# Stacks of the split heads by three transfers to every fourth partition, with zero rows between

## The chip, the cores and the metric

One Trainium2 chip, one NeuronCore. The time is the device time of one execution in microseconds; the median of three runs of the kernel before is 1024.43 us (1022.36 to 1027.62).

## The reference, cut to what matters

The input is 16 sequences of 256 tokens with 128 channels, float32. Two blocks follow each other, each on a layer norm of its input and added back to it: a gated linear attention block with a gated MLP, and a small graph of six attention nodes. The graph is the part that the stacks serve:

```python
for c in range(NUM_NOD):                      # 6 nodes, each reads up to 3 earlier ones
    q = ew[c, 0] * (nodes[in_q] @ We[eq] + be[eq])
    k = ew[c, 1] * (nodes[in_k] @ We[ek] + be[ek])
    v = ew[c, 2] * (nodes[in_v] @ We[ev] + be[ev])
    # _mha: 8 heads of 16 channels, 256 x 256 scores per head and sequence
    scores = jnp.einsum('bqhd,bkhd->bhqk', q @ wq, k @ wk) / jnp.sqrt(dh)
    ctx = jnp.einsum('bhqk,bkhd->bqhd', jax.nn.softmax(scores), v @ wv)
    nodes[c] = act_w[c] * (ctx @ wo) + q
```

## The kernel before

Five engines run hand-ordered programs and meet on semaphores. The first stage, `slots(eng, first, ...)`, does layer norm, linear attention and MLP for the 32 tiles of 128 tokens, four tiles an iteration, eight iterations, overlapped over four (`f`, `i`, `k`, `j`). The second stage, `node_slots(phase)`, does 96 steps, one for each node and sequence (`STEPS`). A step passes through stages at fixed distances in slots: projection of q and k (`a`), scores (`s`, 3 slots later), maxima (`m`, 4), weights (`x`, 5), values and output (`d`, 6). Between the first stage and the steady node stage the first four steps are woven into the last iterations.

**What a stack is.** The products of q and k need more precision than one pass of the float32r type has. So ACT copies q and k with their biases into `qk` (L784, L785), POOL splits each into a high and a low part in `hl` (L591, L594: `K_HI, Q_LO, K_LO, Q_HI`), and SP copies the parts into `st`, where three blocks of 16 channels lie under each other: high by high, high by low, low by high. One matmul over the 48 rows of a half sums the three. There are two halves, partitions 0 to 47 and 64 to 111, of one head each, and four pairs `j` along the free dimension. Partition `64 s + 4 d + j` of `hl` holds channel `d` of head `(j, s)`; a transfer takes the 64 partitions of one half to 16 partitions of `st`, so a stack is six transfers of 128 KB, all issued by SP in `stack` (L506). `st` has `STACKS = 6` buffers of 128 x 2048 float32, `hl` two; `stacked[r]` counts the landings and is awaited by POOL's `split` (two steps later, ahead of L591) and by PE's `scores` (k = 0). PE reads a stack in `scores` and in `weights`, in which a product of `ones` and `mst` of 64 rows subtracts the row maxima first. The matmuls are all recorded at L1292, the helper `mm`.

**The start.** POOL begins with memsets and four loads: `ones`, `mst`, small columns, then `qbd` (L548), `keT` (L549), `kvs` (L550), `am` (L551), each with a semaphore increment; then it waits for `const_in` and casts the identity (L553). Its first work of the first stage is the product of L565. DVE meanwhile takes the statistics of the first four tiles (L919, L1031), adds the epsilons in two tensor-scalars on 128 x 4 (L939, L940), after which ACT takes the inverse roots (L774, L776), DVE refines them and writes the normed rows (L974), and PE transposes them (L1391). PE fills its gaps at the start with dummy products of `ones` (`warm`).

Of the kernel before, what the change touches and what calls it, by code (L numbers as in the profile page):

```python
# [10 lines left out]
F32 = mybir.dt.float32  # L11
# [5 lines left out]
P = 128  # L17
# [20 lines left out]
H, DH = 8, 16  # L38
# [7 lines left out]
JH = H // 2  # L46
HALF = P // 2
PARTS = 3
KROWS = PARTS * DH
MROW = 3  # L50
MCOLS = 2 * MROW * JH
MSTEP = 24
# [6 lines left out]
STACKS = 6  # L59
# [70 lines left out]
def build(nc, a, consts, out):  # L130
    ds = bass.ds
    with ExitStack() as ctx:
# [46 lines left out]
        st = [sb(f"st{r}", [P, JH, 2 * T], F32R) for r in range(STACKS)]  # L179
        hl = [sb(f"hl{n}", [P, 4, T], F32R) for n in range(2)]  # L180
# [114 lines left out]
        def chain(name, events):  # L295
# [4 lines left out]
        L = names("x_first x_half x_in const_in wa_in gk_in wo_in mlp_in cols_in nodew_in wout_in scal_in ln_in")  # L300

        S = names("wa_ok we_t we_c fold_ps fold_ok be_c "
                  "bias_w wz_ok am0 pads_ok eps_ok one_ok ones_ok heads_ok scaled_ok prep_d")

        A = names("xn_ok h_ok hT_ps hT_ok z_ps b_ps eb_ok qkp_ps qke_ok qbd_ok "
                  "v_ps v_ok g_ps eg_ok sg_ok keT_ps keT_ok kv_ps am_ok "
# [22 lines left out]
        stacked = [sem(f"stacked{r}") for r in range(STACKS)]  # L329
# [90 lines left out]
        def unit(k):  # L420

            return k // 2, k % 2
# [45 lines left out]
        @block.sync  # L468
        def _(sp):

            sp.dma_start(xall[:, 0:TPI, :], x_d[:, 0:TPI, :]).then_inc(L["x_first"], 16)
            sp.dma_start(cst[:, :], consts).then_inc(L["const_in"], 16)
            sp.dma_start(wa[:, 0:QK], a["L0_attn_Wq"]).then_inc(L["wa_in"], 16)
            sp.dma_start(wa[:, QK:2 * QK], a["L0_attn_Wk"]).then_inc(L["wa_in"], 16)
            sp.dma_start(wa[:, 2 * QK:2 * QK + D], a["L0_attn_Wv"]).then_inc(L["wa_in"], 16)
            sp.dma_start(wa[:, 2 * QK + D:], a["L0_attn_Wg"]).then_inc(L["wa_in"], 16)
            sp.dma_start(wo[:, :], a["L0_attn_Wo"]).then_inc(L["wo_in"], 16)
            sp.dma_start(wgu[:, 0, :], a["L0_attn_W_gate"]).then_inc(L["mlp_in"], 16)
            sp.dma_start(wgu[:, 1, :], a["L0_attn_W_up"]).then_inc(L["mlp_in"], 16)
            sp.dma_start(wd[:, 0:2, :], a["L0_attn_W_down"][0:256, :].rearrange("(m p) d -> p m d", p=P)).then_inc(L["mlp_in"], 16)  # L480
            sp.dma_start(wd[0:MROWS[2], 2, :], a["L0_attn_W_down"][256:MLP, :]).then_inc(L["mlp_in"], 16)
            sp.dma_start(xall[:, TPI:TILES // 2, :], x_d[:, TPI:TILES // 2, :]).then_inc(L["x_half"], 16)
            sp.dma_start(be_rows, a["L0_ffn_be"]).then_inc(L["nodew_in"], 16)
            sp.dma_start(we_raw, a["L0_ffn_We"].rearrange("e d n -> d e n")).then_inc(L["nodew_in"], 16)
            for j, w in enumerate(("Wq", "Wk", "Wv")):
                sp.dma_start(wqkv_raw[:, j, :, :], a["L0_ffn_" + w].rearrange("c d n -> d c n")).then_inc(L["nodew_in"], 16)
            sp.dma_start(wo_raw, a["L0_ffn_Wo"].rearrange("c d n -> d c n")).then_inc(L["nodew_in"], 16)
            sp.dma_start(xall[:, TILES // 2:, :], x_d[:, TILES // 2:, :]).then_inc(L["x_in"], 16)
            for h in range(H):
                at = VW * (h % GCOL) + DH * (h // GCOL)  # L490
                sp.dma_start(w_out[at:at + DH, :, :], a["L0_ffn_Wo"][:, DH * h:DH * h + DH, :].rearrange("c d n -> d c n")).then_inc(L["wout_in"], 16)


            def stack(a):

                r, old = a.n % STACKS, at_slot(a.n, STACKS)
                if old is not None:
                    sp.wait_ge(B["x_ps"], old.n * UNITS + UNITS)
                for blk, (k, q) in enumerate(((K_HI, Q_HI), (K_HI, Q_LO), (K_LO, Q_HI))):
                    if blk == 0:  # L500
                        sp.wait_ge(B["hi_ok"], a.n + 1)
                    if blk == 1:
                        sp.wait_ge(B["lo_ok"], a.n + 1)
                    for s in range(2):
                        to = HALF * s + DH * blk
                        sp.dma_start(st[r][to:to + DH, :, :].bitcast(F32),  # L506
                                     hl[a.n % 2][HALF * s:HALF * s + HALF, k:q + 1:q - k, :].bitcast(F32))\
                            .then_inc(stacked[r], 16)

            def maxima_rows(m):  # L510

                old = at_slot(m.n, 2)
                if old is not None:
                    sp.wait_ge(B["x_ps"], old.n * UNITS + UNITS)
                else:
                    sp.wait_ge(S["ones_ok"], 3)
                sp.wait_ge(B["mt_ok"], m.n + 1)
                sp.dma_start(mst[m.n % 2][0:(2 * MROW - 1) * MSTEP + 1:MSTEP, :, :], mrows[m.n % 2][:, :]).then_inc(m_in[m.n % 2], 16)

            def phase(t, a, s, m, x, d, z, w, v):  # L520
                if m is not None:
                    maxima_rows(m)
                if at_slot(t, 1) is not None:
                    stack(at_slot(t, 1))

            for t in range(EARLY):
                phase(*stages(t))
            node_slots(phase)
            for f in range(LATE, BATCH):
                for t in range(KT):  # L530
                    sp.wait_ge(E[f - LATE]["done"], t + 1)
                    sp.dma_start(out_d[f][:, t:t + 1, :], xall[:, f * KT + t:f * KT + t + 1, :]).then_inc(B["last_stored"], 16)
            sp.wait_ge(B["last_stored"], 16 * KT * (BATCH - LATE))
# [3 lines left out]
        def _(pool):  # L537
# [11 lines left out]
            pool.memset(keT, 0.0).then_inc(S["pads_ok"], 1)  # L549
            pool.memset(kvs, 0.0).then_inc(S["pads_ok"], 1)  # L550
            pool.memset(am, 0.0).then_inc(S["am0"], 1)  # L551
            pool.wait_ge(L["const_in"], 16)
            pool.tensor_copy(identb[:, :], ident).then_inc(S["ones_ok"], 1)  # L553

# [29 lines left out]
            def split(a):  # L584

                to = hl[a.n % 2]
                old = at_slot(a.n, 2)
                if old is not None:
                    pool.wait_ge(stacked[old.n % STACKS], 96 * old.uses(STACKS))
                pool.wait_ge(B["qk_ok"], a.n + 1)  # L590
                pool.tensor_tensor(to[:, K_HI::Q_HI - K_HI, :], qk[a.n % 2], one_col[:, :].unsqueeze(2).to_broadcast([P, 2, T]), ALU.mult)\  # L591
                    .then_inc(B["hi_ok"], 1)
                pool.wait_ge(B["hi_ok"], a.n + 1)
                pool.tensor_tensor(to[:, K_LO:Q_LO - 1:-1, :], qk[a.n % 2], to[:, K_HI::Q_HI - K_HI, :].bitcast(F32), ALU.subtract)\  # L594
                    .then_inc(B["lo_ok"], 1)
# [694 lines left out]
        def _(pe):  # L1290
# [292 lines left out]
            def scores(s, k):  # L1583

                qt, g = unit(k)
                r = s.n % STACKS
                if k == 0:
                    pe.wait_ge(stacked[r], 96 * s.uses(STACKS))
                if s.n + S_AT < EARLY:
                    if 2 * k + 1 >= len(FIRST_RING):  # L1590
                        pe.wait_ge(B["max_ok"], 2 * k + 2 - len(FIRST_RING))
                else:
                    for e in range(2):
                        banks_free(s.n + S_AT, "s", k, e)
                for n in range(2):
                    for e in range(2):
                        rows, j = slice(HALF * e, HALF * e + KROWS), 2 * g + n
                        i = mm(s_bank(s, k, e)[:, n * T:n * T + T], st[r][rows, j, T + qt * P:T + qt * P + P], st[r][rows, j, 0:T])
                        if n == 1:
                            i.then_inc(B["s_ps"], 1)  # L1600

            def weights(x, k):

                g, kt = unit(k)
                r = x.n % STACKS
                if k == 0:
                    pe.wait_ge(m_in[x.n % 2], 16 * x.uses(2))
                for e in range(2):
                    rows = slice(HALF * e, HALF * e + HALF)
                    banks_free(x.n + X_AT, "x", k, e)  # L1610
                    mm(x_bank(x, k, e)[:, :].rearrange("p (j q) -> p j q", j=2), ones[rows, :], mst[x.n % 2][rows, 2 * g:2 * g + 2, :], stop=False, skip=True)
                for n in range(2):
                    for e in range(2):
                        rows, j = slice(HALF * e, HALF * e + KROWS), 2 * g + n
                        i = mm(x_bank(x, k, e)[:, n * T:n * T + T], st[r][rows, j, kt * P:kt * P + P], st[r][rows, j, T:2 * T],
                               start=False, skip=True)
                        if n == 1:
                            i.then_inc(B["x_ps"], 1)
# [114 lines left out]
```

## Time and profile before

| | us |
|---|---|
| median of 3 runs | 1024.43 |
| the profiled execution | 1026.44 |
| its span, first to last instruction | 1024.6 |
| PE busy | 975.5 |
| DVE busy | 836.5 |
| ACT busy | 724.2 |
| POOL busy | 449.1 |
| mean granted clock of TensorE, of full speed | 0.984 |

The span is what the trace covers; the execution's own time is 1.8 us longer. Busy times overlap, and matmuls are pipelined, so a row's duration is not what one matmul adds. L12 is line 12 of the kernel, PE is TensorE's matmul, PEld its weight load, DVE VectorE, ACT ScalarE, POOL GpSimd, SP the engine that issues the stacks. The first stage lasts until about 250 us, the node stage from there to the end.

### The profile page before, as it was taken

How to read it: one execution, taken by the hardware profiler on the slowest of the kernel's cores; microseconds unless marked ns; L12 is line 12 of the kernel's file. 1: busy time of each engine (PE TensorE's matmuls, PEld its weight loads, DVE VectorE, ACT ScalarE, POOL GpSimd, SP SyncE). 2: the span in 40 equal slices, each digit the busy share in tenths (PEclk: the TensorE clock that was granted, in tenths of full speed). 3: DMA queues.
4: the chain of work that ended last, by engine and by line, in shares of the span. 5: the costliest groups of instructions: out<-in, count | busy, mean ns of one | idle time of the engine just before them, and what ended most of it. 6: DMA issues, size and time to landing. Idle time of an engine off the chain costs nothing.

```text
span 1024.6 us, 26783 instructions
## 1 busy us (share of the span) xinstructions
PE 975.5 (95%) x9705; PEld 698.4 (68%) x9705; DVE 836.5 (82%) x1805; ACT 724.2 (71%) x1602; POOL 449.1 (44%) x874
## 2 busy tenths in 40 slices
PE   7989999998799999999999999999999999999995
PEld 4765656555577777777777777677777777777773
DVE  5466777765689998888888899988888888888896
ACT  3345666655477777787787778878777777787775
POOL 4522222224343334434444348854434435544355
PEclk9889999999899999999999999999999999999998
DMA  9100000003676667767676677876767767767641
GB/s 235 36 1 0 2 0 0 0 1 48 87 111 102 96 100 111 106 106 110 102 111 109 99 113 114 118 110 109 110 99 113 108 101 111 106 105 110 103 70 38
DMA packets 72407, 87.33 MB, mean 85 GB/s; under 512 B 11642, under 2 KB 45950, under 8 KB 72286
## 3 DMA queue, kind: packets, MB, share of 16 engines
q1 hardware_dynamic: 70686, 83.69, 53.1%
q0 software_dynamic: 800, 1.98, 1.1%
q8 instruction: 76, 1.25, 0.7%
q14 instruction: 45, 0.37, 0.2%
q10 hardware_dynamic: 800, 0.05, 0.1%
HBM read 6.90 MB, written 2.10 MB: 9 GB/s over the span
## 4 chain that ended last, share of the span: by engine, by line
PE 75%; DVE 10%; ACT 6%; issue 5%; POOL 3%; DMA 0%; DVEq 0%; ACTq 0%; POOLq 0%
PE bank L1292 73%; ACT region L820 2%; DVE region L1158 1%; DVE region L1090 1%; PE bank L1629 1%; POOL hl L591 1%; DVE region L974 1%; DVE region L1085 1%; POOL out L664 1%; ACT region L796 1%; DVE region L1078 1%; DVE region L1039 1%; DVE region L1070 1%; ACT region L690 0%; DVE region L939 0%
## 5 line engine op out<-in xcount | busy, mean ns | idle before, releaser
L1158 DVE TENSOR_REDUCE region<-bank 128x2 f32<-128x512 f32 x768 | 489.2, 679 | 82.4 <-PE bank L1292 80.6
L820 ACT ACTIVATE region<-bank 128x512 f32<-128x512 f32 x768 | 406.4, 599 | 29.8 <-PE bank L1292 18.6
L1292 PE MATMUL bank<-st 48*128 48x256 f32 x3072 | 310.4, 326 | 5.7 <-DVE region L1158 4.7
L1292 PEld LDWEIGHTS bank<-st 48*128 48x128 f32 x3072 | 243.6, 189 | 20.4 <-DVE region L1158 5.7
L591 POOL TENSOR_TENSOR hl<-qk,one_col 128x512 fp32r<-128x512 f32 x96 | 100.1, 1043 | 358.2 <-ACT qk L785 358.2
L1292 PE MATMUL bank<-region 128*32 128x256 f32 (+3 forms) x3554 | 250.0, 377 | 2.2 <-ACT region L820 0.7
L1292 PEld LDWEIGHTS bank<-region 128*32 128x32 f32 (+2 forms) x3554 | 130.8, 117 | 85.4 <-issue 16.5
L1292 PE MATMUL bank<-mst,ones 64*128 64x512 bf16 x768 | 150.4, 386 | 0.0
L594 POOL TENSOR_TENSOR hl<-qk,hl 128x512 fp32r<-128x512 f32 x96 | 123.7, 1288 | 7.5
L842 ACT ACTIVATE mrows<-bank 24x256 bf16<-24x256 bf16 x96 | 35.8, 373 | 125.9 <-PE bank L1629 125.9
L1292 PEld LDWEIGHTS bank<-mst,ones 64*128 64x128 bf16 x768 | 37.1, 92 | 55.6 <-ACT region L820 26.3
L1165 DVE STREAM_TRANSPOSE cst<-bank 128x512 f32<-128x512 f32 x96 | 67.6, 704 | 6.2 <-PE bank L1292 6.2
L1292 PE MATMUL bank<-xT,w_fold 128*128 128x256 f32 x192 | 63.3, 426 | 0.0
L1292 PE MATMUL bank<-region,w_fold 128*128 128x256 f32 x192 | 56.2, 388 | 0.0
L1292 PE MATMUL bank<-region,w_out 128*128 128x256 f32 x160 | 55.9, 431 | 0.0
L784 ACT ACTIVATE qk<-bank,bcol 128x256 f32<-128x256 f32 x96 | 47.5, 495 | 9.3 <-PE bank L1292 9.3
L1292 PEld LDWEIGHTS bank<-w_fold,region 128*128 128x128 f32 x320 | 47.4, 191 | 3.5
L1292 PE MATMUL bank<-region,wgu 128*128 128x512 f32 (+1 forms) x96 | 47.0, 601 | 2.0 <-DVE region L1085 1.3
L1292 PE MATMUL bank<-w_fold,region 128*128 128x128 f32 x320 | 48.6, 274 | 0.0
L785 ACT ACTIVATE qk<-bank,bcol 128x256 f32<-128x256 f32 x96 | 48.2, 502 | 0.0
L1169 DVE TENSOR_TENSOR region<-cst,region 128x256 f32<-128x256 f32 x96 | 41.0, 427 | 3.3
L834 ACT ACTIVATE region<-bank 128x256 f32<-128x256 f32 x96 | 38.5, 401 | 5.9 <-PE bank L1292 5.9
(194 smaller groups left out, 1267.9 us busy)
## 6 DMA issues: line engine op xcount, KB each, us to landing
st<-hl SPq DMA_DIRECT2D x576, 128.0 KB, 4.4
out<-xall POOLq DMA_DIRECT2D x14, 128.0 KB, 4.1
mst<-mrows SPq DMA_DIRECT2D x96, 12.0 KB
xall<-in_L_attn_hidden_states SPq DMA_DIRECT2D x1, 768.0 KB, 8.2
cst<-in_constants SPq DMA_DIRECT2D x1, 514.5 KB, 4.1
xT<-in_L_ffn_Wq SPq DMA_DIRECT2D x1, 384.0 KB
xT<-in_L_ffn_Wk SPq DMA_DIRECT2D x1, 384.0 KB
xT<-in_L_ffn_Wv SPq DMA_DIRECT2D x1, 384.0 KB
```

What stands on the lines that cost most here:

```text
L591: pool.tensor_tensor(to[:, K_HI::Q_HI - K_HI, :], qk[a.n % 2], one_col[:, :].unsqueeze(2).to_broadcast([P, 2, T]), ALU.mult)\
L594: pool.tensor_tensor(to[:, K_LO:Q_LO - 1:-1, :], qk[a.n % 2], to[:, K_HI::Q_HI - K_HI, :].bitcast(F32), ALU.subtract)\
L664: pool.dma_start(out_d[v.f], xall[:, v.f * KT:v.f * KT + KT, :]).then_inc(B["out_stored"], 16)
L784: act.activation(qk[a.n % 2][:, 0, :], bank[IN][:, 0:T], ACT.Identity, bias=bcol[:, a.c, 1:2])
L785: act.activation(qk[a.n % 2][:, 1, :], bank[IN][:, T:2 * T], ACT.Identity, bias=bcol[:, a.c, 0:1]).then_inc(B["qk_ok"], 1)
L820: act.activation(to, x_bank(x, k, e)[:, :].rearrange("p (j q) -> p j q", j=2), ACT.Exp).then_inc(B["exp_ok"], 1)
L834: act.activation(v[:, :, :, 0:DH], bank[IN][:, 0:T].rearrange("p (k h d) -> p k h d", k=KT, h=H), ACT.Copy).then_inc(B["vals_ok"], 1)
L842: act.activation(mrows[m.n % 2][:, :], bank[IN][0:MCOLS, 0:P].bitcast(BF16), ACT.Copy).then_inc(B["mt_ok"], 1)
L1158: dve.tensor_reduce(mx[s.n % 2][:, to:to + 2], s_bank(s, k, e)[:, :].rearrange("p (j k) -> p j k", j=2), AX_X, ALU.max, negate=True).then_ ...
L1165: dve.transpose(outT, bank[OUT][:, :]).then_inc(B["outT_ok"].sem, 1)
L1169: dve.tensor_tensor(ctxc.rearrange("p (b g d) -> p g b d", g=2, d=DH), blocks[:, :, :, 0:DH], rec.rearrange("p (g b) -> p g b", g=2).unsqu ...
L1292: return pe.matmul(o, w, x, start=start, stop=stop, skip_group_check=skip)
```

## The change

The three blocks of a stack no longer lie under each other. Block `blk` goes to partitions `blk, blk + 4, ..., blk + 124`, so one transfer serves both halves: 128 source partitions of `hl` to 32 partitions of `st`, 256 KB, three of them a stack. Every fourth partition from 3 on is written by none of them; POOL sets all six buffers to zero once, at the start, and SP waits for that ahead of the first use of each buffer. The matmuls run over all 64 rows of a half. The counts of `stacked` fall from 96 to 48 a use. Bytes, `hl` and all else stay.

```diff
-KROWS = PARTS * DH
+STRIDE = PARTS + 1
...
                     sp.wait_ge(B["x_ps"], old.n * UNITS + UNITS)
+                else:
+                    sp.wait_ge(S["zero_ok"], r + 1)
...
-                    for s in range(2):
-                        to = HALF * s + DH * blk
-                        sp.dma_start(st[r][to:to + DH, :, :].bitcast(F32),
-                                     hl[a.n % 2][HALF * s:HALF * s + HALF, k:q + 1:q - k, :].bitcast(F32))\
-                            .then_inc(stacked[r], 16)
+                    sp.dma_start(st[r][blk:P - STRIDE + blk + 1:STRIDE, :, :].bitcast(F32),
+                                 hl[a.n % 2][:, k:q + 1:q - k, :].bitcast(F32)).then_inc(stacked[r], 16)
...
             pool.memset(am, 0.0).then_inc(S["am0"], 1)
+            for r in range(STACKS):
+                pool.memset(st[r][:, :, :].bitcast(F32), 0.0).then_inc(S["zero_ok"], 1)
             pool.wait_ge(L["const_in"], 16)
...
-                    pool.wait_ge(stacked[old.n % STACKS], 96 * old.uses(STACKS))
+                    pool.wait_ge(stacked[old.n % STACKS], 16 * PARTS * old.uses(STACKS))
...
-                    pe.wait_ge(stacked[r], 96 * s.uses(STACKS))
+                    pe.wait_ge(stacked[r], 16 * PARTS * s.uses(STACKS))
...
-                        rows, j = slice(HALF * e, HALF * e + KROWS), 2 * g + n
+                        rows, j = slice(HALF * e, HALF * e + HALF), 2 * g + n
```

The last line is changed in `scores` and in `weights`.

## Rows read from the trace of the kernel before

**Rows 1.** The page: its head, and the chain by engine

```profile
span 1024.6 us, 26783 instructions
...
PE 75%; DVE 10%; ACT 6%; issue 5%; POOL 3%; DMA 0%; DVEq 0%; ACTq 0%; POOLq 0%
```

**Rows 2.** Chain that ended last, 0 to 60 us: start, us, what

```profile
5.32 4.44 DVE region L939
...
9.80 0.22 ACT region L774
...
12.32 0.66 PE bank L1391 x4
...
13.66 1.12 PE bank L1292 x8
...
17.44 1.17 PE bank L1292 x8
```

**Rows 3.** Timeline of POOL at the start: start us, us, engine, line, operation

```profile
5.01 1.82 POOL L548 MEMSET region<- 128x2048 f32 x1
6.75 0.54 POOL L549 MEMSET region<- 128x512 f32 x1
...
7.90 1.83 POOL L551 MEMSET region<- 128x2048 f32 x1
9.66 0.30 POOL L553 CAST identb<-cst 128x128 bf16<-128x128 f32 x1
```

**Rows 4.** Timeline of DVE at the start

```profile
5.32 4.44 DVE L939 TENSOR_SCALAR region<-region 128x4 f32<-128x4 f32 x1
...
21.27 0.17 DVE L939 TENSOR_SCALAR region<-region 128x4 f32<-128x4 f32 x1
```

**Rows 5.** Windows of PE: stretch, length, busy (instructions), granted clock, DMA share, GB/s

```profile
11.50:12.00 0.50, 0.00 (x0) 1.00 1.16 340
...
31.50:32.00 0.50, 0.39 (x4) 0.94 0.00 0
...
42.00:42.50 0.50, 0.50 (x4) 0.82 0.00 0
```

**Rows 6.** Timeline of PE, same work at either clock

```profile
12.81 0.81 PE L1292 MATMUL bank<-ones 128*128 128x512 bf16 x3
...
15.52 1.05 PE L1292 MATMUL bank<-wa,region 128*128 128x128 f32 x8
...
31.61 1.64 PE L1292 MATMUL bank<-wz,region 128*128 128x64 f32 x8 [2.31 <-DVE region L1090]
...
37.66 1.49 PE L1292 MATMUL bank<-ones 128*128 128x512 bf16 x3
...
40.64 1.79 PE L1292 MATMUL bank<-wa,region 128*128 128x128 f32 x8
```

**Rows 7.** Group of the stack's matmuls, PE: busy us, mean ns, idle before

```profile
L1292 PE MATMUL bank<-st 48*128 48x256 f32 x3072 | 310.4, 326 | 5.7 <-DVE region L1158 4.7 <-ACT region L820 1.0
```

**Rows 8.** Groups by line and form, PEld: busy us, mean ns, idle before

```profile
L1292 PEld LDWEIGHTS bank<-st 48*128 48x128 f32 x3072 | 243.6, 189 | 20.4 <-DVE region L1158 5.7 <-issue 3.2 <-ACT region L820 1.5
...
L1292 PEld LDWEIGHTS bank<-wd,region 96*128 96x128 f32 x64 | 7.8, 192 | 0.0
```

**Rows 9.** Timeline of PE in the node stage

```profile
599.87 1.93 PE L1292 MATMUL bank<-region 128*32 128x256 f32 x32
...
606.48 0.39 PE L1292 MATMUL bank<-mst,ones 64*128 64x512 bf16 x2
606.52 1.09 PE L1292 MATMUL bank<-st 48*128 48x256 f32 x12
607.54 1.93 PE L1292 MATMUL bank<-region 128*32 128x256 f32 x32
```

**Rows 10.** The page, DMA issues: size, us from issue to landing

```profile
st<-hl SPq DMA_DIRECT2D x576, 128.0 KB, 4.4
```

**Rows 11.** Longest waits, all engines: us in total, times, longest

```profile
POOL hl L591 <- ACT qk L785: 358.2, 96, 6.7
```

More of the change, by code:

```diff
@@ L302, in build @@
         S = names("wa_ok we_t we_c fold_ps fold_ok be_c "
-                  "bias_w wz_ok am0 pads_ok eps_ok one_ok ones_ok heads_ok scaled_ok prep_d")
+                  "bias_w wz_ok am0 pads_ok eps_ok one_ok ones_ok zero_ok heads_ok scaled_ok prep_d")
         A = names("xn_ok h_ok hT_ps hT_ok z_ps b_ps eb_ok qkp_ps qke_ok qbd_ok "
@@ L1613, in weights @@
                     for e in range(2):
-                        rows, j = slice(HALF * e, HALF * e + KROWS), 2 * g + n
+                        rows, j = slice(HALF * e, HALF * e + HALF), 2 * g + n
                         i = mm(x_bank(x, k, e)[:, n * T:n * T + T], st[r][rows, j, kt * P:kt * P + P], st[r][rows, j, T:2 * T],
```

## The prediction

> **What bounds the kernel now.** I read the page first: of 1024.6 us PE holds 75% of the chain that ended last, DMA 0% [rows 1]. So most of the time is matmul work back to back, and a transfer or an idle engine counts only where this chain touches it. Second, the chain itself in order of time. In the node stage, where the stacks are used, it is PE without a break: a slot, from the start of one step's value products to that of the next, takes 607.54 - 599.87 = 7.67 us [rows 9]. At the start it is not: one DVE instruction of four columns, L939, stands on it for 4.44 us, and ACT's first inverse root, the first transposes and everything after wait for it [rows 2]. Third, the timelines of DVE and POOL over the same microseconds. The same L939 takes 0.17 us one iteration later [rows 4]. The first one begins at 5.32, just after POOL began the first of four memsets that run back to back, and ends at 9.76, when the last of them ends at 9.73 [rows 3, 4]. It was ready at 5.32, so it was held about 4.3 us, through three boundaries between memsets, and got in only where POOL left the run of memsets (L553 comes behind a wait of POOL's own). Fourth, PE's windows at the start, for the clock. Fifth, the groups of the stack's loads and matmuls, and the DMA issues and waits, for what the change touches in the node stage.
>
> **Part 1, six more memsets.** They stand directly behind L551 and ahead of the `const_in` wait, so the run of four becomes a run of ten. Each is 128x2048 f32 like L548 and L551, which last 1.82 and 1.83 us; start to start they take 1.74 (5.01 to 6.75) and 1.76 (7.90 to 9.66) [rows 3]. Six take 6 x 1.75 = 10.5 us, and POOL reaches L553 at 20.2 and not at 9.66.
> On POOL itself this would be free: its next work, the product of L565, comes after DVE's L974, and nothing needs it soon. On DVE it isn't. L939 starts at 5.32 inside the first memset whatever is added behind. If it is held until the run ends, as now, it ends at 9.76 + 10.5 = 20.3. ACT's root waits for it (9.80 [rows 2]), then DVE's rows, then PE's transposes (12.32). The inputs have landed by then and the chain has no other starting point, so nothing absorbs the delay: **+10.5 us**. Bounds: 0 if the hold is not extended (rival 1); 10.5 if it is whole.
> What a page says: the Trainium skill, "SBUF — State Buffer", section "Who interferes with whom", has DVE's two-port operations and GpSimd take one pair of ports, exclusively, "for the whole instruction". Taken as it stands, the second should come in when the first instruction ends: L939 within 1.8 us, by 6.8. Here it came in at 9.76, after four instructions, so the trace is harsher than the page. By the page's rule this change would give rival 1's time.
>
> **Part 2, the clock.** PE has its dummy products until 9.8 and then waits for the transposes. Now it is idle for 2.5 us, to 12.32 [rows 2], and the clock stays at 1.00, that is 2.4 GHz [rows 5]; after the change it is 13 us. In this trace the clock fell to 0.50 (1.2 GHz) at about 31.9, just after PE had done nothing for 2.31 us, and came back at about 42.2 after PE had worked without pause [rows 5, 6]. I expect it low when the transposes begin at 22.8, for about as long. What that costs by the same work at either level: three dummies 1.49 against 0.81, eight products of 128 columns 1.79 against 1.05, eight of 64 columns 1.64 against 1.12: factors of 1.84, 1.70 and 1.46, and I take 1.7 [rows 2, 6]. On the chain lie PE pieces of 0.66, 1.12 and 1.17 us [rows 2]: + 0.7 x 2.95 = 2.1. The three dummies between them: + 0.7. The products that PE does while DVE and ACT work run from 14.8 to 16.57 [rows 6], end 0.87 before the cumulative product at 17.44 [rows 2] and grow by 0.7 x 1.8 = 1.3: + 0.4. Sum **+3.2 us**. By then some ten us have passed since PE resumed. Bounds: above, ten low microseconds of nothing but PE work on the chain, as from 31.9 to 42.2, give 10.3 - 10.3/1.7 = 4.2; below, if that later low stretch falls away because the gaps come at other moments, 3.2 - 4.2 = -1.0.
>
> **Part 3, three transfers for six.** Bytes are the same: 576 of 128 KB [rows 10] become 288 of 256 KB. SP issues half as many, and each covers 128 source and 32 target partitions. Who waits for them? The split on POOL, which has `hl` back only when an older stack has landed, sits idle 358.2 us, each of the 96 times released by ACT's `qk` copy, never by a DMA [rows 11]. PE's scores wait for `stacked` two slots after the issue, and DMA has 0% of the chain [rows 1]. The transfers land in 4.4 us [rows 10] against a slot of 7.67 us [rows 9]. Whatever they gain or lose up to a few us is hidden by PE's own work in those two slots; uncovered it would cost its own size once per slot. Taken: **0**, since no wait is there to be shortened. The new `zero_ok` wait of SP stands ahead of the first six stacks, which belong to the node stage, when the memsets are long past; behind it on SP's queue are only those stacks. 0.
>
> **Part 4, 64 rows for 48.** In the node stage PE is the bound, so this counts 3072 times if at all. A burst of twelve stack matmuls takes 1.09 us although one lasts 326 ns: (1.09 - 0.33) / 5 = 0.15 us a pair, both halves side by side [rows 7, 9]. The row maxima's products, which already have 64 rows in each half, do the same: two of them in 0.39 [rows 9]. So 64 rows don't part the halves. A load lasts 189 ns at 48 rows and 192 at 96 [rows 8]; these loads lie beside matmuls. Bound: 1536 pairs x 1 ns = 1.5 us (a third of the 3 ns); below, nothing is saved, as no row shows fewer rows to be slower. Taken: **0**.
>
> **Sum.** 10.5 + 3.2 = 13.7 us. The profiled execution took 1026.44 us for a span of 1024.6; it becomes 1040.1 for a span of 1038.3. The median of the runs is 2.0 below that execution: 1024.4 + 13.7 = 1038.1.
>
> **Rivals.**
> 1. *DVE gets in between memsets, and the time stays.* The mechanism is that the small DVE operation is let in at the end of a memset, whatever follows it. Against it: three boundaries passed without it [rows 3, 4]. For it: L939 ended within 0.1 us of a memset's end, and a run of ten may be served otherwise than one of four. L939 then ends at 9.8 or earlier, later operations of its kind (the tensor-scalars of L974 and of the weights' scaling) each wait for part of one memset until 20.2: from -3 (L939 in at 6.8) to +5 us, 1026 as the middle. It decides if L939 ends before 12. This is the other side: not slower.
> 2. *The transfers were the limit in disguise and the node stage gets faster.* For it: each of the 96 slots moves 768 KB and depends on them. Against: no DMA on the chain and no break in PE's work. If each slot gave 0.1 us, the time would be 1038.1 - 9.6 = 1028.5 with the start's loss, 1015 without it.
> 3. *64 rows cost PE.* At 6 ns a pair (twice the difference of the loads) 1536 x 6 ns = 9 us: 1047. A mean of the stack's matmuls above 326 ns [rows 7] or slots above 7.67 us would speak for it.
> 4. *The start is delayed and the clock costs nothing, or pays back*: 1034 to 1035. It belongs to the forecast's own range.
>
> **How the numbers follow.** Forecast with its own range 1032 to 1041 (10.5 with -1.0 to +4.2, and 2 either way for the spread of the runs): 0.80. Rival 1: 0.11. Rival 2: 0.04. Rival 3: 0.05. The range of eight in ten is 1031 to 1043.5: below towards the upper end of rival 1, above halfway to rival 3. A measurement here tells about 0.5%, 5.1 us, from no change. Faster by more than that: 0.03 (rival 2 and the best end of rival 1). Within: 0.11. Slower: 0.86.
>
> **What would show it.** In the profile of the changed kernel: L939 at 5.3 lasting 14.9 us and ending with the tenth memset at about 20.3; PE's first transposes at about 22.8 and not 12.32; a granted clock of 0.50 in the windows from there for some 10 us; the node stage begun about 14 us later and lasting the same from its first score to the end; slots of 7.6 to 7.7 us; the stack's matmuls at 326 ns; half as many issues by SP, landing between 3 and 5 us. Wrong would be: L939 short (then rival 1), a slot that is longer or shorter by over 0.05 us (rivals 2, 3), or a start delayed by 10.5 us of which the node stage sees less.

## The result, and the profile after

| | before | after |
|---|---|---|
| median of four runs, us | 1023.39 (1022.29 to 1027.62) | 1036.94 (1035.56 to 1039.26) |
| profiled execution, us (span) | 1026.44 (1024.6) | 1037.09 (1035.0) |
| mean granted clock of the profiled execution | 0.984 | 0.979 |

The changed kernel is slower: ratio 1.0114, 95% interval 1.0089 to 1.0139. Of 1023.39 us that is 11.7 us (9.1 to 14.2). Profiled execution against profiled execution it is 10.65 us. Between the two medians lie 13.55 us, but both rest on four runs, and the runs of one kernel spread over some 6 us (below), so the medians' difference overstates the cost.

Line numbers of DVE, ACT and PE are one higher in the kernel after (L940 was L939), and those of POOL's first four large memsets one lower (L550 was L551). The chain that ended last, 0 to 60 us, start and length, which answers [rows 2]:

```profile
4.87 15.33 DVE region L940
...
22.77 1.11 PE bank L1392 x4
...
29.43 1.17 PE bank L1293 x8
```

The timelines of DVE, POOL and PE at the start [rows 3, 4, 6]:

```profile
4.87 15.33 DVE L940 TENSOR_SCALAR region<-region 128x4 f32<-128x4 f32 x1
```
```profile
9.64 10.53 POOL L552 MEMSET st<- 128x2048 f32 x6
20.10 0.30 POOL L554 CAST identb<-cst 128x128 bf16<-128x128 f32 x1
```
```profile
22.77 1.11 PE L1392 MATMUL bank<-cst,region 128*128 128x128 f32 x4 [13.47 <-DVE region L975]
23.67 1.49 PE L1293 MATMUL bank<-ones 128*128 128x512 bf16 x3
24.95 1.81 PE L1293 MATMUL bank<-wz,region 128*128 128x64 f32 x8
...
28.17 1.05 PE L1293 MATMUL bank<-wa,region 128*128 128x128 f32 x8
29.43 1.16 PE L1293 MATMUL bank<-cst,region 128*128 128x128 f32 x8 [0.20 <-DVE region L1026]
```

One DVE instruction of four columns lasts 15.33 us. It ends at 20.20, where the tenth memset ends (9.64 + 10.53 = 20.17), and not at 9.76. PE stands idle for 13.47 us where it stood for 2.5.

PE's windows, with the granted clock behind the busy time [rows 5]:

```profile
14.00:14.50 0.50, 0.00 (x0) 0.81 0.50 88
27.50:28.00 0.50, 0.50 (x2) 0.54 1.09 260
28.00:28.50 0.50, 0.50 (x4) 1.00 1.29 190
45.00:45.50 0.50, 0.50 (x20) 0.53 0.00 0
51.50:52.00 0.50, 0.50 (x3) 0.65 0.00 0
```

The clock fell while PE was idle, was low when the transposes began, and was back at 28.0, 5.2 us after PE had resumed. A second low stretch runs from 45.0 to 51.8 (6.8 us); its counterpart in before ran from 31.9 to 42.2 (10.2 us).

The node stage: its timeline on PE [rows 9], the groups of the stack's matmuls and loads [rows 7, 8], the DMA issues [rows 10], POOL's wait [rows 11], and the DMA queue that carries the stacks (packets, MB, share of 16 engines), in before and in after:

```profile
601.57 1.06 PE L1293 MATMUL bank<-st 64*128 64x256 f32 x12
602.57 1.93 PE L1293 MATMUL bank<-region 128*32 128x256 f32 x32
...
610.21 0.64 PE L1293 MATMUL bank<-region 128*32 128x256 f32 x8
```
```profile
L1293 PE MATMUL bank<-st 64*128 64x256 f32 x3072 | 310.8, 326 | 5.8 <-DVE region L1159 4.7
...
L1293 PEld LDWEIGHTS bank<-st 64*128 64x128 f32 x3072 | 243.5, 190 | 20.5 <-DVE region L1159 6.0
```
```profile
st<-hl SPq DMA_DIRECT2D x288, 256.0 KB, 2.5
```
```profile
POOL hl L592 <- ACT qk L786: 359.3, 96, 6.7
```
```profile
q1 hardware_dynamic: 70686, 83.69, 53.1%
```
```profile
q1 hardware_dynamic: 66078, 83.68, 23.1%
```

A slot is 610.21 - 602.57 = 7.64 us, as before. A transfer of twice the bytes lands in 2.5 us instead of 4.4, and nobody was waiting for it.

### The profile page after: what moved, and what is told of

Its sections match the earlier page's. It is cut to its first block, busy times and chain, and to the rows that moved or that the text cites. A ratio compares the mean times of both kernels' runs of the same rounds, so it can differ in the third digit from the quotient of the medians.

```text
span 1035.0 us, 26507 instructions
## 1 busy us (share of the span) xinstructions
PE 975.7 (94%) x9705; PEld 698.6 (68%) x9705; DVE 847.4 (82%) x1805; ACT 723.3 (70%) x1602; POOL 458.6 (44%) x880
## 3 DMA queue, kind: packets, MB, share of 16 engines
q1 hardware_dynamic: 66078, 83.68, 23.1%
## 4 chain that ended last, share of the span: by engine, by line
PE 74%; DVE 12%; ACT 6%; issue 5%; POOL 3%; DMA 0%; DVEq 0%; ACTq 0%; POOLq 0%
PE bank L1293 72%; ACT region L821 2%; DVE region L1159 2%; DVE region L940 2%; DVE region L1091 1%; PE bank L1630 1%; POOL hl L592 1%; DVE region L975 1%; DVE region L1086 1%; POOL out L665 1%; ACT region L797 1%; DVE region L1079 1%; DVE region L1071 1%; ACT region L691 0%; ACT L797 0%
## 5 line engine op out<-in xcount | busy, mean ns | idle before, releaser
L1293 PE MATMUL bank<-st 64*128 64x256 f32 x3072 | 310.8, 326 | 5.8 <-DVE region L1159 4.7
L592 POOL TENSOR_TENSOR hl<-qk,one_col 128x512 fp32r<-128x512 f32 x96 | 99.9, 1040 | 359.3 <-ACT qk L786 359.3
L1293 PEld LDWEIGHTS bank<-st 64*128 64x128 f32 x3072 | 243.5, 190 | 20.5 <-DVE region L1159 6.0
```

Source lines behind the costliest of these rows:

```text
L1293: return pe.matmul(o, w, x, start=start, stop=stop, skip_group_check=skip)
```

## The experiments

The theory: the whole loss is the six memsets, since DVE's tensor-scalar of four columns is held until POOL leaves a run of memsets. The questions were which part of the change costs, by what rule DVE is held, what the clock takes, and whether the same reading makes the kernel before faster.

**Which part costs.** `memsets_only` is the kernel before with the six memsets and the wait of SP, the stacks as they were.

```diff
+                else:
+                    sp.wait_ge(S["zero_ok"], r + 1)
...
+            for r in range(STACKS):
+                pool.memset(st[r][:, :, :].bitcast(F32), 0.0).then_inc(S["zero_ok"], 1)
```

> The kernel before with the six memsets and SP's wait for them alone; six transfers, 48 rows. Theory (the memsets extend the run that holds DVE's first tensor-scalar, all else is free): the first tensor-scalar on 128x4 lasts 15 us and ends at 20.2, the first transposes at 22.8, and the whole kernel is as slow as the changed one, 10 to 14 us above the kernel before. Rival (a part of the loss lies in the transfers or the 64 rows): less than 9 us above the kernel before.

Measured: 1037.82 us (four runs) against 1026.61 (23 runs), which is 11.2 us, ratio 1.0110 (1.0078 to 1.0142). DVE's timeline:

```profile
4.90 15.30 DVE L943 TENSOR_SCALAR region<-region 128x4 f32<-128x4 f32 x1
```

`zero_by_dma` is its complement: the kernel after, but the rows that must be zero are written by six transfers of SP from a tile that holds zeros, and `st` has no memset.

```diff
+            sp.wait_ge(S["ones_ok"], 3)
+            for r in range(STACKS):
+                sp.dma_start(st[r][PARTS:P:STRIDE, :, :].bitcast(F32),
+                             mst[0][PARTS:P:STRIDE, :, :]...to_broadcast([P // STRIDE, JH, 2 * T]))\
+                    .then_inc(zeroed[r], 16)
...
-            for r in range(STACKS):
-                pool.memset(st[r][:, :, :].bitcast(F32), 0.0).then_inc(S["zero_ok"], 1)
```

> The changed kernel with its zero rows written by six transfers of SP from the zeroed mst into every fourth partition, and no memset of the stacks. Theory (the loss is only the memsets'): the first tensor-scalar ends at 9.8 as in the kernel before, and the time is within 0.3% of the kernel before: three large transfers and 64 rows are worth nothing. Rival 1 (the transfers gain what nothing showed): faster by 5 us or more. Rival 2 (64 rows cost PE): slower by 5 us or more. Landing of the stacks' transfers 2.5 us in all cases.

Measured: 1024.98 us, ratio 0.9996 (0.9977 to 1.0015). DVE's timeline:

```profile
4.90 4.86 DVE L945 TENSOR_SCALAR region<-region 128x4 f32<-128x4 f32 x1
```

The memsets alone give the loss. The three transfers and the 64 rows together are worth nothing that can be measured, which here means less than about 2 us either way; that they don't cancel each other is read from the slot (7.64 us for 7.67) and from the stack's matmuls (326 ns in both).

**By what rule DVE is held.** `waits_between` is the kernel after with a wait of POOL for each memset behind it, so that its ten memsets are no longer one run.

```diff
-            pool.memset(qbd, 0.0).then_inc(S["pads_ok"], 1)
-            pool.memset(keT, 0.0).then_inc(S["pads_ok"], 1)
-            pool.memset(kvs, 0.0).then_inc(S["pads_ok"], 1)
+            for n, pad in enumerate((qbd, keT, kvs)):
+                pool.memset(pad, 0.0).then_inc(S["pads_ok"], 1)
+                pool.wait_ge(S["pads_ok"], n + 1)
...
+            pool.wait_ge(S["am0"], 1)
             for r in range(STACKS):
                 pool.memset(st[r][:, :, :].bitcast(F32), 0.0).then_inc(S["zero_ok"], 1)
+                pool.wait_ge(S["zero_ok"], r + 1)
```

> The changed kernel with a wait of POOL for its own last memset after each of the ten. Theory A (DVE is let in wherever POOL's run of instructions breaks): the first tensor-scalar ends at about 6.9, at the first break, later ones wait for parts of single memsets, the transposes come at 11 to 13, and the time is within 3 us of the kernel before. Theory B (DVE is let in only when POOL has nothing left to do, or a fixed order serves POOL first): it ends at 20.2 or later and the time stays 10 to 14 us above the kernel before.

Measured: 1026.31 us, ratio 1.0002 (0.9982 to 1.0022). DVE's timeline, then POOL's:

```profile
4.89 1.99 DVE L942 TENSOR_SCALAR region<-region 128x4 f32<-128x4 f32 x1
...
8.43 3.70 DVE L977 TENSOR_SCALAR region<-xall,region 128x128 f32<-128x128 f32 x4
...
12.60 1.32 DVE L1102 TENSOR_SCALAR wa<-wa,cols 128x64 f32<-128x64 f32 x1
```
```profile
8.29 1.81 POOL L550 MEMSET region<- 128x2048 f32 x1
10.15 11.27 POOL L553 MEMSET st<- 128x2048 f32 x6
```

The work on POOL is the same and even ends later (21.42), yet DVE's first tensor-scalar is in at 6.88, at the first break, and each later one waits for at most the memset that runs. What held it is the unbroken run. Beside it the Trainium skill, "SBUF — State Buffer", section "Who interferes with whom", has the loser of the shared ports blocked for the other's instruction. With breaks this trace agrees (1.99 us against a memset of 1.82); without them it doesn't (15.33 us, nine boundaries passed). A wait is not the only thing that ends such a run: in `pads_first` (below) the last memset is followed by the issue of a load, with no wait between, and DVE's tensor-scalar ends there too, at 5.65.

`other_form` is the kernel after with the two instructions of L940 and L941 written as operations with two tensor inputs, both the same column. It leaves out the added constant 1e-11.

```diff
-                    dve.tensor_scalar(ve[:, 0, :], mv[:, :, 1], LN_EPS, None, ALU.add)
+                    dve.scalar_tensor_tensor(ve[:, 0, :], mv[:, :, 1], LN_EPS, mv[:, :, 1], ALU.add, ALU.max)
...
```

> The changed kernel with the two first tensor-scalars written as scalar-tensor-tensor operations with the same column as second input (mv + eps as max of mv + eps and mv; mv times 1 + 1e-6 as mv * 1e-6 + mv), which leaves out the addition of 1e-11 to the second. Theory (only the form that reads one SBUF operand and writes SBUF is held by memsets): they last 0.2 us, end near 5.2, and the next tensor-scalars, the four that write the normed rows, are held to 20.2 in their place and end at 21.3; the transposes come 1.4 us earlier than in the changed kernel. Rival (any DVE work on SBUF is held): the first one still lasts until 20.2.

Measured: one time of 1037.13 us, span 1035.1. DVE's timeline:

```profile
5.00 0.16 DVE L940 SCALAR_TENSOR_TENSOR region<-region 128x4 f32<-128x4 f32 x1
...
8.18 0.16 DVE L973 TENSOR_TENSOR region<-region 128x4 f32<-128x4 f32 x1
8.26 12.56 DVE L975 TENSOR_SCALAR region<-xall,region 128x128 f32<-128x128 f32 x4
```

Inside the same memsets the other form takes 0.16 us, and so do the tensor-tensor operations behind it. The first tensor-scalar after them, L975, takes over the wait and ends at 20.82. So it is the form that is held, not DVE. The transposes came at 20.88, 1.89 us before those of after (I had expected 1.4). The span shows none of it. The later low stretch of the clock ran from about 42.3 to 52.5, 10.2 us for 6.8, which goes the same way; one run can't tell more:

```profile
42.00:42.50 0.50, 0.50 (x7) 0.79 0.00 0
...
52.50:53.00 0.50, 0.50 (x5) 0.97 0.00 0
```

`memsets_late` is the kernel after with the six memsets behind POOL's first product of the first step.

```diff
-            for r in range(STACKS):
-                pool.memset(st[r][:, :, :].bitcast(F32), 0.0).then_inc(S["zero_ok"], 1)
...
+                    if isinstance(i, int) and i == 0:
+                        for r in range(STACKS):
+                            pool.memset(st[r][:, :, :].bitcast(F32), 0.0).then_inc(S["zero_ok"], 1)
```

> The changed kernel with the six memsets behind POOL's first product (the one that begins at 12.4 in the kernel before), where POOL has 16 us with nothing to do. The first tensor-scalar then ends at 9.8. Theory A (a run of POOL's instructions without a break holds DVE's tensor-scalars, whatever begins the run): the two that scale wa, asked for at 12.4 while that product runs, are held to about 24, PE's products with wa come some 10 us late, and the time is 8 to 12 us above the kernel before. Theory B (an operation of DVE that is already asking gets in between two instructions of different kinds): they end by 14, the tensor-scalar of the second iteration at 21.3 is held to 24, and the time is 0 to 3 us above the kernel before.

Measured: 1028.34 us against 1024.89 (29 runs), ratio 1.0037 (1.0012 to 1.0062). One of its ten runs took 1038.04, the others 1024.54 to 1030.01; that one was not profiled, so whether DVE was held to the run's end in it is not known. DVE's timeline, then POOL's:

```profile
12.38 4.61 DVE L1101 TENSOR_SCALAR wa<-wa,cols 128x64 f32<-128x64 f32 x1
13.44 3.73 DVE L1102 TENSOR_SCALAR wa<-wa,cols 128x320 f32<-128x320 f32 x1
```
```profile
13.41 10.74 POOL L567 MEMSET st<- 128x2048 f32 x6
...
16.90 2.01 POOL L567 MEMSET st<- 128x2048 f32 x1
```

Neither theory had this. The scalings waited for the product and two memsets and got in at 16.9, in the middle of a run without a wait of POOL; the memset that began there lasts 2.01 us where the others last 1.80, so it was the one that stood back. The unbroken run at the start held DVE to its end in every profile, and this one did not. The time is 3.5 us above before, near theory B's, but by another mechanism. The second scaling began at 13.44, when the product ended, so the product and then the memsets held them. What opened the run at 16.9 is not settled.

**What the clock takes.** `dummies_fill` is the kernel after with 66 dummy products at the start in place of 8, so that PE is not idle before the transposes.

```diff
-            warm(8)
+            warm(66)
```

> The changed kernel with 66 dummy products of PE for 8 behind the small product at the start, so that PE works until about 21.7 and not 9.3. Nothing else changes. Theory (the rest of the loss at the start is the low clock after PE's long pause): the granted clock stays at 1.00 until the transposes at 22.8, and from there to the cumulative product PE needs 5.1 us as in the kernel before (12.32 to 17.44) and not 6.7 (22.77 to 29.43), a gain of 1.5 us there; the whole time 0 to 4 us below the changed kernel. Rival (the clock is not what costs there): the cumulative product stays at 29.4.

Measured: 1035.07 us, ratio 1.0086 (1.0057 to 1.0116). PE's timeline, then its windows:

```profile
22.79 0.66 PE L1392 MATMUL bank<-cst,region 128*128 128x128 f32 x4 [0.77 <-DVE region L975]
...
27.90 1.16 PE L1293 MATMUL bank<-cst,region 128*128 128x128 f32 x8 [0.86 <-DVE region L1026]
```
```profile
42.00:42.50 0.50, 0.44 (x2) 0.50 0.00 0
52.00:52.50 0.50, 0.50 (x6) 0.82 0.00 0
```

From the transposes to the cumulative product it takes 5.11 us, as before (5.12), against 6.66 in after: the low clock there costs 1.55 us. But a later stretch, 41.9 to 52.2, is low for 10.2 us instead of 6.8, and the profiled span is 1035.3 for 1035.0. Of its four runs two have a mean clock of 0.989 and take 1032.6 and 1032.8, two have 0.983 and 0.984 and take 1037.4 and 1037.5. In the profiled run the next stretch took back what the first had saved; the two runs at 0.989 have no profile and may have kept it. The medians (1035.07 for 1036.94) don't decide: each rests on four runs, and the kernel before itself has 1026.61 in the set of 23 and 1024.89 in the set of 29 that stand beside these runs.

**Whether the reading makes before faster.** `pads_first` is the kernel before with POOL's start in another order: the small pads and the four memsets that can hold DVE come first, then POOL's four loads; the memsets of `mst` move behind the scaling of the node weights.

```diff
-            for n in range(2):
-                pool.memset(mst[n][:, :, :], 0.0).then_inc(S["ones_ok"], 1)
-            pool.dma_start(scal[:, 0:18], a["L0_ffn_ew"].rearrange("a b -> (a b)").partition_broadcast(P)).then_inc(L["scal_in"], 16)
...
             pool.memset(am, 0.0).then_inc(S["am0"], 1)
+            pool.dma_start(scal[:, 0:18], a["L0_ffn_ew"].rearrange("a b -> (a b)").partition_broadcast(P)).then_inc(L["scal_in"], 16)
...
+                for n in range(2):
+                    pool.memset(mst[n][:, :, :], 0.0).then_inc(S["ones_ok"], 1)
```

> The kernel before (six transfers, 48 rows, no memset of the stacks) with POOL's start in another order: the memsets of qbd, keT, kvs and am directly behind ones, then the four loads; the memsets of mst go to the end of POOL's work on the weights, near 43 us. Theory (DVE's first tensor-scalar waits for the end of POOL's run of memsets): the run ends near 5.7, the tensor-scalar too and not at 9.8, the transposes come when PE has done its dummies, at about 9.9 and not 12.3, and the scaling of wz, which needs columns that land at about 12.3, limits the gain to 1 us: 0 to 3 us below the kernel before. Rival (POOL's loads hold it as well): it ends near 8.2.

Measured: 1022.49 us (twelve runs) against 1024.89 (29 runs), ratio 0.9961 (0.9945 to 0.9978). DVE's timeline, POOL's, and ACT's:

```profile
4.98 0.67 DVE L939 TENSOR_SCALAR region<-region 128x4 f32<-128x4 f32 x1
...
9.76 0.27 DVE L1097 TENSOR_SCALAR wz<-bank,cols 128x64 f32<-128x64 f32 x1
```
```profile
0.93 1.81 POOL L542 MEMSET region<- 128x2048 f32 x1
...
3.82 1.81 POOL L545 MEMSET region<- 128x2048 f32 x1
5.57 0.71 POOL L546 DMA_DIRECT2D scal<-in_L_ffn_ew  x1
```
```profile
7.22 0.27 ACT L683 ACTIVATE region<-bank 16x128 f32<-16x128 f32 x1 [0.93 <-PE bank L1303]
7.39 0.19 ACT L774 ACTIVATE region<-region 128x8 f32<-128x8 f32 x1
```

The same rule, used the other way: L939 lasts 0.67 us and ends at 5.65, the run of memsets ends at 5.63, the transposes come at 9.90 instead of 12.32, and the first matmul of a stack at 252.6 instead of 254.8. Of the 4.1 us that DVE gained, ACT takes back 1.7: its roots stand behind a copy that waits for PE. By the interval it is 2 to 6 us faster than before, and its median is the lowest of this study. I had put the limit at 12.3 us, for the landing of the gate columns; the scaling that needs them began at 9.76 with no wait.

`start_ordered` adds two edits to it: two dummies for eight, and a semaphore of its own for the one column that DVE's scaling of `wz` needs (it waited for all six).

```diff
-                dve.wait_ge(L["cols_in"], 16 * 6)
+                dve.wait_ge(L["col0_in"], 16)
...
-            warm(8)
+            warm(2)
```

> As pads_first, with two more edits: two dummy products for eight behind the small product, so that PE is free at about 8.3, and a semaphore of its own for the first of the columns, which lands by 6, so that the scaling of wz waits for that alone. Theory: transposes at about 8.4, scaling of wz at 8.4 and not 12.2, everything behind it about 4 us earlier: 2.5 to 5 us below the kernel before. Rival (something else, a landing of weights or of the constants, is late next): less than 1 us below it.

Measured: 1022.90 us (twelve runs), ratio 0.9975 (0.9956 to 0.9994). ACT's timeline:

```profile
7.35 0.27 ACT L683 ACTIVATE region<-bank 16x128 f32<-16x128 f32 x1 [1.05 <-PE bank L1304]
7.52 0.19 ACT L774 ACTIVATE region<-region 128x8 f32<-128x8 f32 x1
```

My theory failed: the roots came at 7.52 and the transposes at 10.08, not at 8.4, and no earlier than in `pads_first`. The time is 2.0 us below before, under the theory's 2.5 and over the rival's 1. The two edits bring nothing that shows; ACT's copy is still ahead of the roots.

## Why the prediction was right, point by point

**Part 1, the memsets: right.** I wrote that L939 would begin at 5.3, last 14.9 and end at about 20.3. It began at 4.87 (the input landed 0.45 us earlier in this execution, which moved the end by nothing), lasted 15.33 and ended at 20.20, 10.44 us later than before; the transposes came at 22.77 for the expected 22.8. `memsets_only` reproduces it, `zero_by_dma` takes it away, `waits_between` shows that the unbroken run is what holds. Two things the forecast did not name. I had placed the start of L939 inside the first large memset, but in after it began 0.14 us ahead of it (4.87 against 5.01), while POOL was ending the issue of its last load, and it was held all the same; nine boundaries passed, and not three. And the scaling of `wa` (L1099, in after L1100) meets POOL's product: it began 0.04 us ahead of the product in before and took 1.13 us, and 0.05 us ahead of it in after and took 0.24, while the product took 1.39 us instead of 1.03. So which of two that begin together is served first was not the same in the two profiles, and no run here shows what decides it. That is off the chain.

**Part 2, the clock: the mechanism was right, the term was too large.** I took 3.2 us, on the assumption that the clock stays low for some ten microseconds after PE resumes, as from 31.9 to 42.2 in before. It was back after 5.2. From the transposes to the cumulative product it takes 29.43 - 22.77 = 6.66 us against 5.12 [rows 2], +1.54. The later stretch was then shorter by 3.4 us and gave that back: where the product of `wz` begins the delay is 43.59 - 31.61 = 11.98 us, and at the first matmul of a stack it is 264.9 - 254.8 = 10.1. So the term's total in the profiled executions is about 0 (10.65 us less the 10.44 of L939), inside my bounds of -1.0 to 4.2; I had named the lower bound's cause (the later stretch changes) but not given it the weight.

**Part 3, the transfers: 0, right.** The landing went from 4.4 to 2.5 us, outside the 3 to 5 that I had expected, and the busy share of the DMA engines for that queue from 53.1% to 23.1%. POOL's wait is still 96 times released by ACT, 359.3 us for 358.2. A transfer that is hidden in two slots of 7.64 us brings nothing by landing 1.9 us sooner. Rival 2 falls: `zero_by_dma` has the faster transfers without the loss at the start, and its ratio is 0.9996.

**Part 4, the rows: 0, right.** 326 ns a matmul and 190 a load for 326 and 189; a slot of 7.64 us for 7.67. Rival 3 falls.

**The node stage** begins 10.1 us later, not 14, which is the clock's term again; from the first matmul of a stack to the end of the span it takes 770.1 us for 769.8.

**The sum.** For the profiled execution I had 1040.1 us, and it was 1037.09: 3.0 too many, which is the clock's 3.2. That the forecast for the median is off by only 1.2 us (1038.1 for 1036.94) is in part luck of which runs were drawn: the four of before lie low. Against the 23 runs of before that `memsets_only` had beside it, after lies 10.3 us higher and `memsets_only` 11.2.

**Rival 1** was half right about the chip and wrong about this kernel: DVE does get in between memsets when there is a break (`waits_between`) and once without one (`memsets_late`), but not in this run of ten. That the hold of four memsets would extend to ten was a guess from one row; it held in the three profiles of such a run at the start (after, `memsets_only`, `other_form`), and `memsets_late` shows that it need not have.

## What to carry to other kernels

A zeroing memset on GpSimd is not free because GpSimd has time: look which DVE instructions start while it runs, and whether they are tensor-scalars. A run of memsets without a break between them can hold such an instruction, however small, to the run's end; break the run, let a DMA write the zeros, or put the run where DVE has nothing of that form to do (this last was not tried here). A faster transfer is worth what someone waits for it: look for the wait before counting the gain.

## What the runs showed of the hardware that I had not expected

- **The form decides.** On the same 128x4 column inside the same memsets a tensor-scalar took 15.33 us and an operation with two tensor inputs 0.16. The Trainium skill, "SBUF — State Buffer", section "Who interferes with whom", says that a DVE instruction with two SBUF inputs contends with a GpSimd instruction that reads SBUF, not with one that only writes it. A memset only writes, and the trace agrees.
- **A stack lands faster by three transfers over more partitions.** 128 KB into 16 partitions in a row took 4.4 us, six at a time; 256 KB into every fourth partition took 2.5, three at a time. SP needed 4.14 us to issue a stack and now 1.93. The Trainium skill, "SBUF — State Buffer", section "Door 1: The DMA port swizzle", has the bandwidth depend on how many ports the partitions reach, and by its table 16 in a row reach 4 and every fourth of 128 reaches 16. The direction agrees; how much of it is the ports and how much the halved number of transfers no run here parts. What else is under way has a share: the 14 transfers of `out`, which the change doesn't touch, land faster too (between 2.3 and 5.5 us in before, between 2.3 and 3.9 in after; the last number of these rows, of before and of after, is the median):

```profile
out<-xall POOLq DMA_DIRECT2D x14, 128.0 KB, 4.1
```
```profile
out<-xall POOLq DMA_DIRECT2D x14, 128.0 KB, 2.4
```

- **Runs of one kernel differ with the clock.** The 29 runs of before lie from 1022.2 to 1028.6 us, in order of their mean granted clock: 0.987 at 1022.2 to 1023.2, 0.985 at 1023.2 to 1024.3, 0.984 at 1024.8 to 1026.1, 0.982 at 1027.2 to 1027.7, 0.980 at 1028.5 to 1028.6. The low stretches at the start fall differently from profile to profile, even behind the same gap. PE stood idle for 2.3 to 2.5 us ahead of the first transposes (12.3) in before, in `zero_by_dma` and in `memsets_late`. In before the clock stayed at 1.00 there; in `zero_by_dma` it was 0.50 from 12.9 to 16.3, in `memsets_late` from 13.3 to 20.2. So a gap in one profile doesn't forecast where the clock will be low in the next, and a gain of 1.5 us at one stretch (`dummies_fill`) can be lost at another.
